# The last expert's output through one-hot products, a woven order, and up products of 256 and 384 slots

## What is computed

```python
# layer 2, mixture of experts: N = 2048 tokens, K = 2 of E = 8 experts, capacity 640
logits = x @ Wg.T
top_v, top_i = jax.lax.top_k(logits, K)
gates = jax.nn.softmax(top_v, axis=-1)
...
exp_batches = zeros((E, cap, d)).at[flat_e, pos_safe].set(x[tok], mode='drop')
h = jnp.einsum('ecd,edf->ecf', exp_batches, W1)
inp, gate = jnp.split(h, 2, axis=-1)
h = jax.nn.gelu(inp, approximate=False) * gate
exp_out = jnp.einsum('eci,eid->ecd', h, W2)
gathered = exp_out[flat_e, jnp.minimum(pos_safe, cap - 1)]
contrib = jnp.where(keep, gates_f, 0.0)[:, None] * gathered
out = jax.ops.segment_sum(contrib, tok, num_segments=N)
# layer 3: per batch row two picked MLPs and a shared one (256 -> 1024 -> 256, gated by gelu)
```

## Time and profile before

| | us |
|---|---|
| runs | 1010.43, 1009.55, 1008.32; median 1009.55 |
| the profiled execution | 1008.6, its span from the first to the last instruction 1007.4 |
| TensorE | busy 953.5 of the span (95%), mean granted clock 0.993 |
| VectorE, ScalarE, GpSimd | busy 497.4, 436.1, 272.2 |
| experts, from the first up product to the end of the last down product | 280.66 to 472.1 |
| from there to the fourth tile's successor in the MLP | 472.08 to 503.16 |

### The profile page before, as it was taken

One profiled execution on the slowest core, in us unless ns is written; L12 is line 12 of the kernel. 1 busy time (PEld: TensorE's weight loads), 2 busy tenths in 40 slices (PEclk: granted clock), 3 DMA queues, 4 the chain that ended last, 5 costly groups with the idle time before them and its releaser, 6 DMA issues.

```text
span 1007.4 us, 13258 instructions
## 1 busy us (share of the span) xinstructions
PE 953.5 (95%) x4952; PEld 783.0 (78%) x4952; DVE 497.4 (49%) x947; ACT 436.1 (43%) x820; POOL 272.2 (27%) x243
## 2 busy tenths in 40 slices
PE   5989999999899999999699999999999999998998
PEld 2667767787589999987587788888888888876786
DVE  5645453566444554544467433333333333688544
ACT  2555564523154444544234334244343342326675
POOL 1333221402256555536452014023041140100000
PEclk9999999999999999999999999999999999999999
DMA  7130001102325444441521300302003003000011
GB/s 261 43 106 21 22 1 64 73 22 84 122 47 125 133 114 133 115 152 35 190 57 39 126 1 1 126 0 110 16 1 126 1 0 126 1 1 1 1 42 43
DMA packets 21648, 67.48 MB, mean 67 GB/s; under 512 B 4497, under 2 KB 11921, under 8 KB 19281
## 3 DMA queue, kind: packets, MB, share of 16 engines
q1 hardware_dynamic: 16592, 39.88, 11.2%
q0 software_dynamic: 4704, 26.49, 9.3%
q10 hardware_dynamic: 288, 0.26, 0.1%
HBM read 55.09 MB, written 9.44 MB: 64 GB/s over the span
## 4 chain that ended last, share of the span: by engine, by line
PE 72%; DVE 12%; ACT 6%; issue 4%; DMA 3%; another core or an unknown queue 1%; SPq 1%; DVEq 0%; ACTq 0%; POOLq 0%
PE banks L934 15%; PE banks L936 14%; PE banks L935 14%; PE banks L1132 4%; PE banks L1133 4%; PE banks L1131 4%; PE banks L1014 3%; PE banks L998 2%; PE banks L1181 1%; PE banks L1180 1%; PE banks L1167 1%; PE banks L1168 1%; PE banks L950 1%; PE banks L1005 1%; DMA expert_output<-y_rows 1%
## 5 line engine op out<-in xcount | busy, mean ns | idle before, releaser
L934 PE MATMUL banks<-input_hi,mlp_hi 128*128 128x512 f32 (+1 forms) x396 | 156.1, 394 | 3.9 <-DVE input_lo L1741 2.4
L936 PE MATMUL banks<-input_hi,mlp_lo 128*128 128x512 f32 (+1 forms) x396 | 155.3, 392 | 0.0
L935 PE MATMUL banks<-input_lo,mlp_hi 128*128 128x512 f32 (+1 forms) x396 | 154.8, 391 | 0.0
L1937 POOL TENSOR_TENSOR mlp_lo<-weight_stage,mlp_hi 128x768 fp32r<-128x768 f32 x40 | 73.6, 1841 | 241.8 <-ACT mlp_hi L1369 241.8
L1384 ACT CAST hidden_hi<-hidden 128x512 fp32r<-128x512 f32 x96 | 59.6, 621 | 176.4 <-DVE hidden L1751 108.0
L1757 DVE TENSOR_TENSOR hidden_lo<-hidden,hidden_hi 128x512 fp32r<-128x512 f32 x96 | 66.5, 693 | 71.3 <-ACT hidden_hi L1384 71.3
L1751 DVE SCALAR_TENSOR_TENSOR hidden<-banks,L_expert_weight,gelu 128x512 f32<-128x512 f32 x64 | 48.0, 751 | 97.6 <-PE banks L936 97.4
L1907 POOL TENSOR_TENSOR ffn_w_lo<-weight_stage,ffn_w_hi 128x512 fp32r<-128x512 f32 x48 | 62.0, 1294 | 109.2 <-ACT ffn_w_hi L1331 109.2
L934 PEld LDWEIGHTS banks<-input_hi,mlp_hi 128*128 128x128 f32 x396 | 75.2, 190 | 20.2 <-issue 4.3
L936 PEld LDWEIGHTS banks<-input_hi,mlp_lo 128*128 128x128 f32 x396 | 75.3, 190 | 16.4
L935 PEld LDWEIGHTS banks<-input_lo,mlp_hi 128*128 128x128 f32 x396 | 75.5, 191 | 16.0
(11 more groups left out here) (298 smaller groups left out, 2099.2 us busy)
## 6 DMA issues: line engine op xcount, KB each, us to landing
weight_stage<-in_packF SPq DMA_DIRECT2D x8, 1536.0 KB, 6.9
weight_stage<-in_shared SPq DMA_DIRECT2D x2, 3072.0 KB, 10.9
expert_output<-y_rows SPq DMA_DIRECT2D x40, 128.0 KB
weight_stage<-in_cond_w SPq DMA_DIRECT2D x4, 512.0 KB, 6.4
residual<-in_xT SPq DMA_DIRECT2D x4, 512.0 KB, 10.7
first_half_swapped<-first_half SPq DMA_DIRECT2D x32, 64.0 KB, 2.0
routed_input<-x_rows SPq DMA_DIRECT2D x16, 128.0 KB, 1.8
weight_stage<-in_ffn_w SPq DMA_DIRECT2D x2, 1024.0 KB, 6.8
```

What stands on the lines that cost most here:

```text
L934: pe.matmul(o, wh, dh, start=(i == 0), stop=False)
L935: pe.matmul(o, wh, dl, start=False, stop=False)
L936: last = pe.matmul(o, wl, dh, start=False, stop=(i == len(terms) - 1))
L1937: pool.tensor_tensor(wDl[s][:, qs], stage[:, qs], f(wDh[s][:, qs]), ALU.subtract).then_inc(done)
```

## The change

It has four parts that meet around the experts.

1. **Widths.** The 640 slots go as 256 and 384 (`SPLIT`, `WIDTHS`) in place of 320 and 320. The first half of an expert now needs two turned-in tiles in place of three.
2. **Woven order.** In `up_expert` the step's `yield` stands between the product with the gelu and the hi copy, so what is woven in comes between ACT's gelu and its hi copy. The first picked MLP's weights are gathered in two halves, each as soon as one half of the staging buffer is free, one beside expert 5 and one beside expert 6; the split of a piece is first a copy into the lo's place (`wm_pre` on ACT), the subtraction in place (POOL, two pieces on DVE), and later the hi copy, when the memory of expert 6's weights is free: 8 more copies of 768 columns on ACT.
3. **One-hot products.** For the first 512 tokens the output of expert 7 doesn't go through DRAM. Each slot gets its gate (a table in DRAM, gathered by slot), ACT and DVE split the gated rows (`hot_hi`, `hot_lo`), and 20 products of 512 columns with the matrix "slot is of token" (`onehot` on DVE, beside expert 6) add them in place (`hot`). The rows of the other experts for tiles 0 to 3 are fetched, combined and added by TensorE to the same two banks beside expert 7. `hot_add`, `hot_in`, `hot_in_lo` then make the first 512 columns of the MLP's input at once; `early_half` goes, and the first two steps take their products in another order (`first_products`).
4. **Spins.** 16, 13 and twice 4 around the first gathers in place of 8 and 27; the 30 and 7 after the experts go, and 4 stand before the first MLP.

```diff
-HALF = CAP // 2
-FIRST_HALF = -(-HALF // P)
+FIRST_HALF = 2
+SPLIT = FIRST_HALF * P
+WIDTHS = SPLIT, CAP - SPLIT
...
-SPIN = {"first scores": 12, "logits": 5, "slots": 8, "first rows": 27, "first tile": 30, "next tile": 7}
+SPIN = {"first scores": 12, "logits": 5, "slots": 16, "first rows": 13, "next rows": 4, "first hidden": 4}
...
-        if e + 1 == G:
-            pool.append(("ld_mlp", 0))
+        if e + 2 >= G:
+            pool.append(("ld_mlp", 0, e + 2 - G))
...
                 act.append(("gelu0", e, h, i))
                 dve.append(("prod1", e, h, i))
+                yield
                 act.append(("he_hi", e, h, i))
                 dve.append(("he_lo", e, h, i))
-                yield
+                if (e, h, i) == (G - 2, 1, IT - 1):
+                    mlp_piece(2)
...
+            if e == G - 1:
+                act.append(("hot_hi", j))
+                dve.append(("hot_lo", j))
             dve.append(("yrow", e, j))
+            if e == G - 3 and j >= 3:
+                mlp_piece(j - 3)
+            if e == G - 2:
+                dve.append(("onehot", j))
+                if j < 3:
+                    act.append(("wm_hi", 0, j))
+                if j == 1:
+                    mlp_piece(3)
+                if j == 3:
+                    mlp_piece(4)
+                if j == 4:
+                    mlp_piece(6)
+                    mlp_piece(5)
...
+    def beside_last_expert():
+        mlp_piece(7)
+        for tt in range(QT):
+            pool.append(("fetch", tt))
+        yield
+        for step in range(1, 8):
+            if step <= 5:
+                act.append(("wm_hi", 0, step + 2))
+            if 4 <= step <= 6:
+                dve.append(("comb", step - 4))
+            if step == 6:
+                banks["yt", 0] = (HOT, HOT + 1)
+                pe.append(("yt", 0))
+            if step == 7:
+                pe.append(("yt", 1))
+            yield
+        pe.append(("yt", 2))
+        yield
+        dve.append(("comb", 3))
+        yield
+        yield
+        pe.append(("yt", 3))
+        yield
...
     gather(0)
-    spin(SPIN["first rows"], 6)
-    run(turn_in(0, 0, FIRST_HALF))
+    for j in range(FIRST_HALF):
+        spin(SPIN["next rows" if j else "first rows"], 6)
+        run(turn_in(0, j, j + 1))
+    spin(SPIN["next rows"], 6)
...
+    for j in range(ST):
+        pe.append(("hot", j))
+    for k in range(KD):
+        dve.append(("hot_add", k))
+        act.append(("hot_in", k))
+    for k in range(KD):
+        dve.append(("hot_in_lo", k))
+    spin(SPIN["first hidden"], 6)
...
+        def first_products(o, terms, s):
+            for k, (wh, wl, dh, dl) in enumerate(terms):
+                pe.wait_ge(*ready("hot_in", k))
+                pe.matmul(o, wh, dh, start=(k == 0), stop=False)
+                pe.matmul(o, wl, dh, start=False, stop=False)
+            for k, (wh, wl, dh, dl) in enumerate(terms):
+                pe.wait_ge(*ready("hot_in_lo", k))
+                last = pe.matmul(o, wh, dl, start=False, stop=(k == KD - 1))
+            last.then_inc(s)
...
+            elif kind == "hot":
+                j, = key
...
+                pe.wait_ge(*ready("hot_lo", j))
+                for k in range(KD):
+                    ks = slice(k * P, (k + 1) * P)
+                    pe.matmul(banks[:, HOT + k, :], y7H[:, j, ks], hot[:, j, :], start=False, stop=False)
+                    last = pe.matmul(banks[:, HOT + k, :], y7L[:, j, ks], hot[:, j, :], start=False, stop=(j == ST - 1))
```

261 lines of the change are left out of this document (181 added, 80 removed).

## The result

| | us | beside the kernel before |
|---|---|---|
| the kernel changed | 995.09 median (994.62 to 996.63, 4 runs) | ratio 0.986, 95% interval 0.984 to 0.988 |
| the kernel before, same chip | 1009.41 median (1008.32 to 1010.43, 4 runs) | |
| its profiled execution | 994.62, span 993.4, clock 0.997 | 1008.6, 1007.4, 0.993 |

Times of variants are medians of undisturbed runs; one run of all_cures_equal, 2411.86 us, is left out for that.

A forecast was written before the change was run, and what follows sets the result against it. TensorE, busy 95% of the span, was taken as the bound, with time to gain at idle places and half clock. From 1008.6 us: -5.5 + 0.2 - 3.2 - 14.9 + 0.4 = -23.0, so 985.6 us; range 979 to 995.

The forecast's parts named there:

- Start: Start of the experts: rows land 2.82 us after issue, first up product at 276.5, half clock behind it gone; -5.5 us.
- Widths: Up products: turns of 384 columns 0.174 to 0.175 us apart, so 256 and 384 cost +0.2 us over twice 320.
- Experts 0 to 6: Middle experts: TensorE hardly waits, POOL's idle time covers the five gate gathers and ramp; 0 us.
- DVE locked out by POOL: Rival, chance 0.05: two lo's in the last expert each held for a whole POOL piece, +3.1 us, 988.7 us.
- the gap: From T, the last down product's end, to the MLP: first product T + 6.25, first dn ended T + 16.2; -14.9 us.
- Woven order: Experts 0 to 6: gains nothing by itself, lets the 256-wide half work; ACT's turn 1.3 to 1.4 us, was 1.93.
- Slower: Rival, chance 0.04: narrow half starves TensorE, ACT 2.0 us behind per expert plus half clock, +5 us on before, 1013.6.
- The last expert: Expert 7: half loads land 6.9 us after issue, prod1 hardly waited for, near 24 us instead of 27.53; -3.2 us.
- The combine's +0.4: MLP: combining starts a step later, so one more step holds a tile and a second-MLP piece; +0.4 us.
- The worst case: Whole kernel: start -1.4, last expert 0, gap -12.4, given as 994.6 us.

The follow-up runs named there:

- all_cures_equal: Changed kernel at 320 and 320, pieces 0 and 1 on DVE, gate gathers split over experts 3 and 4, expert 1's gathers singly between expert 0's pieces: 989.4 us, 0.984.
- gates_spread: Changed kernel with the five gate gathers issued one each behind the gathers of experts 2 to 6 instead of all in expert 3: 1002.48 us, 1.005.
- lo_burst: Kernel before, POOL's pieces for expert 4 held until ACT's fourth hi piece, then in a run with no gather ahead: 998.71 us against 998.2.
- order_undone: Changed kernel with the step's yield put back behind ACT's hi and DVE's lo: 1008.81 us, 1.003 of before.
- train_then_run: Kernel before, expert 4's five gathers in one train beside expert 3's up products, full-width pieces right behind: 1009.42 us against 1005.75.

## Why the prediction was wrong

**Start: right.** First up product at 275.69 (forecast 276.5), the first rows landing 2.8 us after issue. Of the 5.0 us, 0.85 came from an earlier shift; from first gather to first up product it was 9.6 us and is 5.5. But the half clock didn't go: signals late in expert 0 idled TensorE 1.96 us, and it fell anyway. Without late signals expert 0 takes 24.0 us at clock 1.00, so the term holds there.

**Widths: right.** Turns of 384 columns are 0.174 to 0.176 us apart, and experts 4 and 5 take 22.4 us.

**"Experts 0 to 6": this step failed.** It costed at 0 what POOL got in addition, the gate gathers, and let the two pieces and five gathers ahead of the splits of expert 6 only put off a load. I took "POOL stands idle for longer than that in each expert" for cover, and it was, for the mean: POOL is busy 12.65 of 22.38 us. It isn't cover where the additions stand in a row. Two pieces ahead of five gathers put the end of the last gather 8.3 us into expert 6, where before it had been 1.6 us ahead of it, and five pieces became one run. +7.0 us in expert 6. Part of the 7.0 is the late signals' and a wait of 0.49 for `y_rows`: on a chip without late signals a still longer lock (6.89, gates_spread) leaves expert 6 at 28.1 us, 5.7 above 22.4.

**The rival *DVE locked out by POOL*: misread.** The two cases I had weighed were 0.3 us and 1.84 us a piece, with a chance of 0.05 and a price of 3.1, put in the last expert. The lock came in the expert before and spanned the run: 5.71 us. I took the lo of 0.81 us at 453.58 to speak against a lock for a whole piece. The piece beside it says the opposite:

```profile
452.23 1.83 POOL L1937 TENSOR_TENSOR mlp_lo<-weight_stage,mlp_hi 128x768 fp32r<-128x768 f32 x1 [13.61 <-ACT mlp_hi L1369]
```

It ends at 454.06. The lo came 1.36 us into it, so only 0.47 of the piece was left, and the lo ended 0.33 behind it: it was held for what was left. The lo's beside single pieces of the changed kernel end 0.3 to 0.4 us behind the piece too, whenever they began; the longest, 1.17 and 1.18 us, began 0.4 into a piece of 1.3. The Trainium skill ("SBUF — State Buffer", shared port pair) says that a GpSimd operation holds the pair for a whole instruction and the other engine blocks fully. The trace agrees, in the kernel before already. A hold for one instruction doesn't give 5.71 us, though: here it lasted to the end of a run of five.

**Late signals: missed.** Some 5.6 us in expert 0 (29.57 against 24.0 on a chip without them) and 2.0 in expert 3. Nothing in my reading of before looked for them, though its own waits hide some: 3.29 and 2.38 us in the gap. On the chip of lo_burst that gap is 26.00 us, not 31.08, so 5 of the 14.9 us are gained only on chips with late signals. That the gap's forecast came out to 0.1 us says nothing on them.

**Woven order: worth more than forecast, and not for the reason given.** I had it gain "nothing by itself" in experts 0 to 6 and only let "the 256-wide half work". order_undone shows some 8 us of worth there. But the narrow half works without it too: experts 4 and 5 take 22.6 and 22.4 us, since ACT's lag of 1.4 us stays inside the buffered steps and is caught up in the wide half. The turn with the order is 1.59 to 1.65, not the 1.3 to 1.4 of the forecast. So that order_undone lies 3 us above before, where the rival *Slower* had 5, is luck: its 2.0 us in every expert didn't come. What the order saves lies in experts 0 to 3 and 6, and in the last; how it does so there isn't shown.

**The last expert and the gap: right.** 23.62 us (about 24 forecast), the halves landing 7.2 us after their issue; first MLP product at T + 6.24 (6.25), first `dn` ended at T + 16.20 (16.2). The combine's +0.4 may lie in the rest of 0.7, which wasn't taken apart.

**Sum.** 985.6 forecast; +7.0 (expert 6, mostly the lock) +5.6 +2.0 (late signals); -0.8 and -0.7 since the start and the last expert gained more, +0.3 in the rest; and -4.4, which is what is left over and which I put down to waits and half clock of before in experts 0 to 6 that went and that I had not counted: 994.6, as profiled.

The worst case in the prediction is added up wrong: -1.4 and -12.4 from 1008.6 give 994.8, not 994.6, and with the +0.2 and +0.4 of the sum 995.4. That it comes near the measured 995.1 is chance: it supposes a poor start and a poor last expert, and both did better than forecast.

## What to carry to other kernels

An engine's idle share covers added work only if its place in the order leaves a gap where its consumers are due: write down what the engine has in a row there, not what it has per stage. A stretch in which GpSimd is late costs twice, by the wait itself and by the run that follows, in which VectorE's operations that read only SBUF stand still. Keep a wait of GpSimd between its gathers and a run of its two-input operations. When a row is to speak for or against a lock, look at when the other engine's operation began and ended, not at how long the row is. And price a change on more than one chip before crediting a gap that late signals had widened.

## What the runs showed of the hardware

- A VectorE operation that reads only SBUF, begun beside a GpSimd subtraction, ends when that subtraction has ended: a cast of five columns 1.83 us beside 1.85, an operation of two columns 1.16 in place of 0.16, a lo 0.3 to 0.4 us behind the piece. `prod1`, with one input from PSUM, was never held: at most 0.56 us in all 659 cases beside a piece.
- A run of GpSimd subtractions directly behind its indirect gathers shuts out a VectorE subtraction with two SBUF inputs to the run's end (3.35 to 7.27 us, eight cases, at 256, 320 and 384 columns), at 1.24 us a piece. Behind a pause of GpSimd VectorE gets in between pieces of 512 columns (1.49 us at most), at 1.38 to 1.47 us a piece; single pieces directly behind a gather held a lo to 1.60 us.
- On some chips TensorE's signals come late, often in clumps, by up to 4.7 us: in the first experts, beside transposes and down products, behind trains of gathers and in the gap. Spreading one train took one clump away, in one profile; a train of five in train_then_run made none. In all ten profiles with late signals records of the up products' semaphore are missing as well, 375 to 384 of 385 are there; in the seven without none is missing. So the recording itself may have a part in it. What sets it, and why other chips never show it, stays open.
